# One pair of head sums taken by VectorE alone, and the order of several steps moved, in a gated cross-attention and low-rank expert layer

## The chip, the core and the metric

The kernel runs on one core of a Trainium2 chip. The metric is the device time of the whole program in microseconds. The engines are called as the profile calls them: PE (TensorE, matrix products), DVE (VectorE), ACT (ScalarE), POOL (GpSimd), SP (SyncE, which here only issues DMAs).

## What is computed

16 batches x of 128 rows and 1024 columns go through two gated residual steps. C is 128, there are 8 heads of 64 channels, and the second step has 64 experts of rank 16.

```
n = 1024 columns; xn = layernorm(x); q, k, v projections with Wq, Wk, Wv of 512 x 128
qh = softmax(Wq xn, over the 64 channels of a head) * 64**-0.5
kh = softmax(Wk ctx, over the 1024 columns)
context = kh vh^T (64 x 64 per head);  out = Wo (context^T qh) + bo
x = x + tanh(g_xattn) * out / max(norm(out over channels), 1e-12) * g * sqrt(128)
u = layernorm(x);  scores = u Wr^T;  gates = softmax(top 16 of 64 scores), else 0
h = u A^T (64 x 16);  x = x + tanh(g_ffn) * ((h * gates) B^T) * 2
```

## The kernel before, in words

**Precision.** A float32 product is done as three passes (`three_pass`): both operands are split in a high part (suffix `_hi`, copied by ACT in a rounded type) and a low part (`_lo`, the difference, made by DVE or POOL); lines L61, L62 and L63 are the passes hi x hi, hi x lo and lo x hi. A "512-column matmul" below is one such pass of 512 columns.

**Attention part.** It is a software pipeline of 17 bodies, b = 0 to 16. Body b does the head of batch b (query and key projections in `mm_q` and `mm_k`, the two softmaxes, the transposes of both) and the tail of batch b-1 (context, fold with the weights Wv and Wo, output). Body 15 has no batch to prepare ahead, body 16 only has a tail. Each engine has its own program, written out by hand in `body`, and the engines meet at semaphores only; so the order in each engine's `body` is the order of its work. DVE runs bodies 0 and 1, a loop over 2 to 4 (with `early=True`, where `part_early(b - 2)` adds up squares for the norm), a loop over 5 to 13, and bodies 14, 15 and 16.

**Query softmax.** The 1024 values of a row (position) of a batch, in four pairs p of 128 positions x 1024 (two groups of eight heads by 64 channels), go through these steps: DVE `max_q` (L1013) takes the maximum of each head straight from PE's result, for p = 0, 1, 2 PE subtracts it by a matmul (`shift_q`, L1491), ACT `exp_q` makes `qe` (L678; p = 3 in L685 pieces with the maximum as a bias), POOL `halve` adds the two halves of each head (`qhalf`, L447), DVE `sum_q` reduces these 32 values per head (`qsum`, L1018) and takes the reciprocal (`qrec`, L1021), POOL multiplies (L454), PE transposes (`tr_q`, L1510), ACT and DVE split the transposed tile (`hi_q`, `lo_q`, L693 and L1027). Keys: `max_k` (L1007), `exp_k` (L670), `tr_k` (L1501), `hi_k` (L700), `lo_k` (L1038).

**Tail.** `context` (PE) gives kc; `hi_kc` (ACT) and `lo_kc` (DVE, L1043) split it; `fold` (PE) needs `kc_lo`; `scale_m` (DVE, L1055) scales; `mt_hi` (ACT), `mt_lo` (POOL, L546); `output` (PE) needs `mt_lo` and `qT_lo`; `out_o` (ACT, L728) copies out. In body 0 there is also the fold of the output weights: `wvo_hi` (ACT, L867) and `wvo_lo` (DVE, L1304), each in two copies. `spread` (DVE, L1003) broadcasts the row norms by a transpose, `stats2_sums` (L1071, L1073) and `std2` make the second layer norm's mean and deviation of a batch.

**FFN part.** Fifteen bodies, b = 1 to 15 (`ffn_body`), each with `up(b)` (72 passes), the column sums of a later batch (`sum_u`, L1566, from DVE's `part`), and `down(b-1)`. DVE's work around them: `norm_steps` (11 small steps of an inverse square root for the output norm), `lo_moved_h`, `turn_y` (transpose `u_in`), `route` in 11 `route_step`s (top 16 of the scores and their softmax; step 2 releases ACT's `exp_scores`, L811), `gated` and `turn_h` (L1145, L1178). ACT then moves strips (`y_raw`, `h_raw`, L778, 32x256 each), and POOL does the residual addition from `rb` (L525, L528). The third body (`third`, b = 3) has an order of its own in DVE's program.

## Time and profile before

| | |
|---|---|
| Time, median of 3 runs | 920.5 us (919.33 to 921.06) |
| The profiled execution | 921.38 us |
| Its span, first to last instruction | 919.5 us |
| Mean granted TensorE clock | 0.996 |
| PE busy (share of the span) | 898.3 us (98%) |
| DVE, ACT, POOL busy | 737.2 (80%), 680.6 (74%), 520.1 (57%) |
| Chain that ended last, by engine | PE 63%, DVE 16%, ACT 7%, issue 7%, POOL 5% |

How to read it: the share of an engine is over the whole span. PE is 98% busy, so about 21 us of the span are time in which PE waits, in some fifteen places; every other engine has much more idle time, which costs nothing as long as PE is not waiting for it. The timeline rows below give start, length, engine, source line, operation, tiles and shapes, and in brackets how long the engine was idle before and who released it.

### The profile page before, as it was taken

Reading aid. Unit: us, or ns where it says so; the run is one execution under the profiler, and the core shown is the slowest. Engines: PE = TensorE matmul, PEld = TensorE weight load, DVE = VectorE, ACT = ScalarE, POOL = GpSimd, SP = SyncE. Lnnn points to the kernel's source line nnn. Section 1 sums busy time; section 2 is a strip of 40 time slices with the busy share of each in tenths; the row PEclk is TensorE's granted clock in tenths of the full one; section 3 lists DMA queues with packets and bytes.
Section 4 is the critical chain, followed back from the end, with each engine's and each line's share of the span. In section 5 each row is a group of like instructions: output and inputs, shape, how many; then the busy total and the mean of one; then the engine's idle time right before and its main releaser. Section 6 shows DMA issues by size and latency. Waiting matters only on the chain.

```text
span 919.5 us, 15914 instructions
## 1 busy us (share of the span) xinstructions
PE 898.3 (98%) x4732; PEld 760.7 (83%) x4732; DVE 737.2 (80%) x1531; ACT 680.6 (74%) x1392; POOL 520.1 (57%) x342
## 2 busy tenths in 40 slices
PE   7899999999999999999999999999999999999998
PEld 5687887878888888888887799988899989999996
DVE  6888899888888888888887878897877768777642
ACT  4787787687678768777877748678888878888731
POOL 3686777788798789879778958231222212222100
PEclk9999999999999999999999999999999999999999
DMA  4323524443453544344232694112222111212001
GB/s 160 115 82 129 178 78 156 163 144 111 161 185 108 168 139 127 109 135 156 91 115 69 207 354 165 67 68 69 76 71 70 67 64 69 70 67 69 24 24 46
DMA packets 35325, 104.09 MB, mean 113 GB/s; under 512 B 4432, under 2 KB 11600, under 8 KB 35280
## 3 DMA queue, kind: packets, MB, share of 16 engines
q1 hardware_dynamic: 29520, 82.59, 26.2%
q0 software_dynamic: 5472, 20.45, 7.5%
q10 hardware_dynamic: 288, 0.52, 0.1%
q8 instruction: 19, 0.31, 0.1%
q14 instruction: 26, 0.21, 0.1%
HBM read 79.43 MB, written 24.12 MB: 113 GB/s over the span
## 4 chain that ended last, share of the span: by engine, by line
PE 63%; DVE 16%; issue 7%; ACT 7%; POOL 5%; DMA 1%; ACTq 0%; DVEq 0%; POOLq 0%
PE ps L61 19%; PE ps L63 18%; PE ps L62 18%; PE ps L1501 4%; PE ps L1510 3%; DVE qmax L1013 2%; ACT h_raw L778 2%; DVE kmax L1007 2%; PE ps L1491 2%; DVE qT_lo L1027 1%; DVE mt L1055 1%; ACT y_raw L778 1%; ACT qT_hi L693 1%; POOL x L528 1%; POOL qe L454 1%
## 5 line engine op out<-in xcount | busy, mean ns | idle before, releaser
L525 POOL TENSOR_TENSOR rb<-u_in,rb 128x1024 f32<-128x1024 f32 x14 | 33.7, 2410 | 219.0 <-DVE rb L1003 219.0
L454 POOL TENSOR_TENSOR qe<-qe,qrec 128x1024 f32<-128x1024 f32 x64 | 121.2, 1903 | 28.9 <-DVE qrec L1021 28.9
L61 PE MATMUL ps<-aT_hi,yT_hi 128*128 128x448 f32 (+2 forms) x360 | 119.9, 333 | 1.8 <-DVE hg L1145 1.3
L62 PE MATMUL ps<-aT_hi,yT_lo 128*128 128x448 f32 (+2 forms) x360 | 118.7, 330 | 0.0
L63 PE MATMUL ps<-aT_lo,yT_hi 128*128 128x448 f32 (+2 forms) x360 | 118.6, 330 | 0.0
L1027 DVE TENSOR_TENSOR qT_lo<-ps,qT_hi 128x512 fp32r<-128x512 f32 x128 | 82.1, 683 | 42.6 <-ACT qT_hi L693 42.6
L778 ACT ACTIVATE h_raw<-hg 32x256 f32<-32x256 f32 x248 | 103.0, 415 | 17.0 <-DVE hg L1178 14.2
L447 POOL TENSOR_TENSOR qhalf<-qe 128x512 f32<-128x512 f32 x64 | 82.3, 1286 | 32.7 <-ACT qe L685 30.8
L778 ACT ACTIVATE y_raw<-u_in 32x256 f32<-32x256 f32 x216 | 89.5, 414 | 5.8 <-DVE u_in L1161 3.5
L61 PE MATMUL ps<-bT_hi,hT_hi 128*128 128x512 f32 x240 | 93.7, 390 | 0.0
L62 PE MATMUL ps<-bT_hi,hT_lo 128*128 128x512 f32 x240 | 93.5, 390 | 0.0
L63 PE MATMUL ps<-bT_lo,hT_hi 128*128 128x512 f32 x240 | 93.4, 389 | 0.0
L678 ACT ACTIVATE qe<-ps 128x1024 f32<-128x1024 f32 x48 | 49.2, 1025 | 46.4 <-PE ps L1491 46.4
L693 ACT ACTIVATE qT_hi<-ps 128x512 fp32r<-128x512 f32 x128 | 70.7, 598 | 14.9 <-PE ps L1510 13.6
L1007 DVE TENSOR_REDUCE kmax<-ps 128x1 f32<-128x1024 f32 x64 | 77.9, 1216 | 4.0 <-PE ps L63 2.4
L670 ACT ACTIVATE ek<-ps,kmax 128x1024 f32<-128x1024 f32 x64 | 72.3, 1130 | 4.7 <-DVE kmax L1007 3.0
L61 PEld LDWEIGHTS ps<-aT_hi,yT_hi 128*128 128x128 f32 x360 | 68.5, 190 | 5.0 <-issue 1.7
L1510 PE MATMUL ps<-ident,qe 128*128 128x128 f32 x512 | 69.1, 275 | 1.7 <-DVE ekT_lo L1038 1.5
L62 PEld LDWEIGHTS ps<-aT_hi,yT_lo 128*128 128x128 f32 x360 | 68.4, 190 | 2.1
L63 PEld LDWEIGHTS ps<-aT_lo,yT_hi 128*128 128x128 f32 x360 | 68.5, 190 | 1.8
L1510 PEld LDWEIGHTS ps<-ident,qe 128*128 128x128 f32 x512 | 58.0, 140 | 14.0 <-DVE ekT_lo L1038 3.3
L700 ACT ACTIVATE ekT_hi<-ps 128x512 fp32r<-128x512 f32 x100 | 54.5, 601 | 16.0 <-PE ps L1501 16.0
(180 smaller groups left out, 2556.3 us busy)
## 6 DMA issues: line engine op xcount, KB each, us to landing
x_in<-in_x SPq DMA_DIRECT2D x16, 512.0 KB, 4.2
ctx_in<-in_ctx SPq DMA_DIRECT2D x16, 512.0 KB, 4.7
ctxT_in<-in_ctxT SPq DMA_DIRECT2D x16, 512.0 KB, 3.3
ctxT_hi<-in_ctxT POOLq DMA_DIRECT2D x16, 512.0 KB, 3.7
u_scratch<-osb SPq DMA_DIRECT2D x16, 512.0 KB, 2.9
x<-in_x SPq DMA_DIRECT2D x15, 512.0 KB, 4.0
out<-res SPq DMA_DIRECT2D x15, 512.0 KB, 2.9
turn_scratch<-ek SPq DMA_DIRECT2D x14, 512.0 KB, 5.7
```

The source lines that it names most:

```text
L61: nc.tensor.matmul(psum, whi, mhi, start=start, stop=False)
L62: nc.tensor.matmul(psum, wlo, mhi, start=False, stop=False)
L63: return nc.tensor.matmul(psum, whi, mlo, start=False, stop=stop)
L447: nc.gpsimd.tensor_tensor(qhalf[:, p % 2, :].rearrange("p (h d) -> p h d", d=DH // 2), v[:, :, 0:DH // 2], v[:, :, DH // 2:DH], ALU.add).t ...
L454: nc.gpsimd.tensor_tensor(v, v, w, ALU.mult).then_inc(q_norm, 1)
L670: nc.scalar.activation(to, of, ACT.Exp, bias=kmax[:, j:j + 1], accum_out=ksum[:, j:j + 1]).then_inc(k_exp, 1)
L693: nc.scalar.activation(qT[0][:, :, n * P:n * P + P], psT[:, h, :].rearrange("p (j n) -> p j n", n=P), ACT.Copy).then_inc(q_hi, 1)
L700: nc.scalar.activation(ekT[0][:, 4 * h:4 * h + 4, j * P:j * P + P], psT[:, h, :].rearrange("p (n d) -> p n d", d=P), ACT.Copy).then_inc(k_ ...
L778: last = nc.scalar.activation(dst[32 * q:32 * q + 32, 256 * a:256 * a + 256], src[32 * a:32 * a + 32, 256 * q:256 * q + 256], ACT.Copy)
L1007: nc.vector.tensor_reduce(kmax[:, j:j + 1], psK, axis=AX.XY, op=ALU.max, negate=True).then_inc(k_max, 1)
L1027: nc.vector.tensor_tensor(qT[1][:, :, v], psT[:, h, :].rearrange("p (j n) -> p j n", n=P), qT[0][:, :, v].bitcast(f32), ALU.subtract).then ...
L1510: last = nc.tensor.transpose(psT[:, h, j * P:j * P + P], qe[:, p, w:w + P], ident[:, :])
```

## The change

It has seven parts.

1. POOL's `halve(b-1, 3)` is gone; DVE's `sum_q` for p = 3 reduces the 1024 exponentials in `qe` itself, once it has them from ACT, in place of 512 half sums.
2. In DVE's bodies 1 to 14, `sum_q(b-1, 3)` stays in its place, `max_q(b, 0)` comes ahead of `lo_kc(b-1)`, and `early_guess` (body 14 only) behind `max_q`. In the loop over bodies 2 to 4 `part_early` moves from behind `lo_k(b, 1)` to behind `max_k(b, 1)`. Body 1 has no `part_early`.
3. In body 0, ACT's `wvo_hi` goes behind `exp_q(0, 2)`, and DVE's `wvo_lo` (`low_fold`) behind `lo_k(0, 2)`, ahead of `max_q(0, 3)`.
4. In body 15, both `spread`s, `sum_q(14, 3)` and `stats2_sums(0, 0)` move on DVE, and `scale_first` and `normalise(0, 0)` on ACT; the latter goes to body 16.
5. In body 16 `sum_q` comes ahead of `lo_kc`, and PE does `tr_q(15, 1)` ahead of `tr_y(0, 0)`.
6. In body 14 PE's `sum_early` comes behind both halves of `context`.
7. In DVE's third FFN body the first three steps of `route(3)` go to the front and all eleven steps of the next norm behind `turn_y(4, 0)`.

The core of the diff (the pieces are in this order: POOL's body; ACT's body; DVE's sum, body and FFN body; PE's body 16, then its others):

```diff
-                if tail:
-                    halve(b - 1, 3)
...
             def body(b, head, tail, ahead, early=False):
                 if tail:
                     exp_q(b - 1, 3)
+                if tail and not head:
+                    normalise(0, 0)
                 if head:
                     hi_xn(b, 1)
+                if tail:
+                    hi_kc(b - 1)
                 if head and not ahead:
                     scale_first(0)
-                if tail:
-                    hi_kc(b - 1)
...
+                if head:
+                    hi_k(b, 1)
+                    exp_k(b, 3)
+                if tail:
+                    hi_q(b - 1, 3)
                 if head and not ahead:
                     scale_first(1)
-                if head:
+                if tail and head:
+                    out_o(b - 1, 0, early)
+                if head:
+                    exp_q(b, 2)
                     if not started(b):
                         act.wait_ge(fold_done, 1)
...
-                    hi_k(b, 1)
-                    exp_k(b, 3)
-                if tail:
-                    hi_q(b - 1, 3)
-                    if head:
-                        out_o(b - 1, 0, early)
-                if head:
-                    exp_q(b, 2)
...
             def sum_q(b, p):
-                dve.wait_ge(q_half, 4 * b + p + 1)
-                nc.vector.tensor_reduce(qsum[:, p, :], qhalf[:, p % 2, :].rearrange("p (h d) -> p h d", d=DH // 2),
-                                        axis=AX.X, op=ALU.add).then_inc(q_sum, 1)
+                if p == 3:
+                    dve.wait_ge(q_exp, 8 * b + 8)
+                    whole = qe[:, 3, :].rearrange("p (h d) -> p h d", d=DH)
+                else:
+                    dve.wait_ge(q_half, 3 * b + p + 1)
+                    whole = qhalf[:, p % 2, :].rearrange("p (h d) -> p h d", d=DH // 2)
+                nc.vector.tensor_reduce(qsum[:, p, :], whole, axis=AX.X, op=ALU.add).then_inc(q_sum, 1)
...
                 if ahead and started(b):
                     stats(b + 1)
-                if norms:
-                    early_guess()
                 if ahead and started(b):
                     std(b + 1, range(3))
-                if tail and ahead:
-                    sum_q(b - 1, 3)
                 if tail:
-                    lo_kc(b - 1)
-                if tail and not head:
                     sum_q(b - 1, 3)
                 if head and started(b):
                     max_q(b, 0)
+                if norms:
+                    early_guess()
+                if tail:
+                    lo_kc(b - 1)
+                if head and started(b):
                     max_k(b, 1)
-                if last:
-                    sum_q(b - 1, 3)
-                if last:
-                    dve.wait_ge(ctx_lo, 2 * NB)
-                    spread(0, rb_first[0], n_newton, 4 * NEWTON)
+                if early:
+                    part_early(b - 2)
...
                 if tail:
                     scale_m(b - 1)
+                if last:
+                    dve.wait_ge(ctx_lo, 2 * NB)
+                    spread(0, rb_first[0], n_newton, 4 * NEWTON)
...
-                if last:
-                    dve.wait_ge(xn_lo, 2 * NB)
-                    spread(1, rb_first[1], n_newton, 4 * NEWTON)
-                if early:
-                    part_early(b - 2)
...
+                if last:
+                    dve.wait_ge(xn_lo, 2 * NB)
+                    spread(1, rb_first[1], n_newton, 4 * NEWTON)
                 if ahead:
                     max_k(b + 1, 0)
+                if head and not last:
+                    sum_q(b, 1)
+                if head:
+                    lo_k(b, 2)
+                if not started(b):
+                    low_fold()
                 if last:
                     stats2_sums(0, 0)
-                if head:
                     sum_q(b, 1)
-                    lo_k(b, 2)
...
                 elif third:
-                    norm_steps(5, range(7))
+                    for n in range(3):
+                        route_step(3, n)
                     lo_moved_h(2)
                     turn_y(4, 0)
-                    norm_steps(5, range(7, NRT))
-                    route(3)
+                    norm_steps(5, range(NRT))
+                    for n in range(3, TOP):
+                        route_step(3, n)
                     spread_u(5)
...
-                    tr_y(0, 0)
                     tr_q(b - 1, 1, next(turn))
+                    tr_y(0, 0)
...
-                if isinstance(b, int) and b == NB - 2:
-                    sum_early()
                 if tail:
                     context(b - 1, 0)
                     context(b - 1, 1)
+                if isinstance(b, int) and b == NB - 2:
+                    sum_early()
```

How it moves instructions, at three places. First the loop over bodies 2 to 4 on DVE, from the last sum of the batch before to the first transposed query tile (rows of register and wait instructions are left out). Before:

```order
L1018 TENSOR_REDUCE qsum<-qhalf 128x16
L1021 RECIPROCAL qrec<-qsum 128x16
L1043 TENSOR_TENSOR kc_lo<-ps,kc_hi 128x512
L1013 TENSOR_REDUCE qmax<-ps 128x16
L1007 TENSOR_REDUCE kmax<-ps 128x1
L1027 TENSOR_TENSOR qT_lo<-ps,qT_hi 128x4x128
...
L969 TENSOR_REDUCE part<-osq 128x32
```

Now:

```order
L1021 TENSOR_REDUCE qsum<-qe 128x16
L1023 RECIPROCAL qrec<-qsum 128x16
L1011 TENSOR_REDUCE qmax<-ps 128x16
L1045 TENSOR_TENSOR kc_lo<-ps,kc_hi 128x512
L1005 TENSOR_REDUCE kmax<-ps 128x1
L967 TENSOR_REDUCE part<-osq 128x32
L1029 TENSOR_TENSOR qT_lo<-ps,qT_hi 128x4x128
```

The maximum stands ahead of `kc_lo`, the sum reads `qe`, and `part` (which stood some 35 rows further down, behind `ekT_lo`) now stands between the key maximum and `qT_lo`. In the loop over bodies 5 to 13 the rows are the same without `part`.

The second place is DVE in body 15, from the fourth query pair's transposed tile to the third key tile's low part (`rb_first1` is the broadcast of the second norm, `bn2` and `mv2` are `stats2_sums`). Before:

```order
L1003 STREAM_TRANSPOSE rb_first1_101<-nr_86 128x1024
L1027 TENSOR_TENSOR qT_lo_68<-ps,qT_hi_67 128x4x128 x2
L1323 RECIPROCAL krec<-ksum 128x4
L1071 BN_STATS bn2<-x2_0_105 128x6 x2
L1073 BN_AGGR mv2<-bn2 128x2
L1018 TENSOR_REDUCE qsum<-qhalf_73 128x16
L1021 RECIPROCAL qrec<-qsum 128x16
L1038 TENSOR_TENSOR ekT_lo_66<-ps,ekT_hi_65 128x4x128 x2
L76 TENSOR_SCALAR s1<-mv2 128x1
```

Now:

```order
L1029 TENSOR_TENSOR qT_lo_68<-ps,qT_hi_67 128x4x128 x2
L1322 RECIPROCAL krec<-ksum 128x4
L1001 STREAM_TRANSPOSE rb_first1_101<-nr_86 128x1024
L1040 TENSOR_TENSOR ekT_lo_66<-ps,ekT_hi_65 128x4x128 x2
L1083 BN_STATS bn2<-x2_0_105 128x6 x2
L1085 BN_AGGR mv2<-bn2 128x2
L1021 TENSOR_REDUCE qsum<-qhalf_73 128x16
L1023 RECIPROCAL qrec<-qsum 128x16
L76 TENSOR_SCALAR s1<-mv2 128x1
```

The broadcast stands behind `qT_lo` and `krec`, and the statistics and the sum behind `ekT_lo`.

The third place is DVE at the start of the third FFN body (`sc`, `top8` and `neg_top` are the first three steps of the routing, `ns`, `nr` and `nt` those of the norm). Before:

```order
L984 TENSOR_TENSOR nt_87<-nr_86,ns_85 128x32
L986 SCALAR_TENSOR_TENSOR nt_87<-nt_87,nr_86 128x32
L1191 TENSOR_TENSOR hT_lo_114<-h_raw_117,hT_hi_113 128x1024
L1161 STREAM_TRANSPOSE u_in0_103<-u_in0_103 128x1024
L988 SCALAR_TENSOR_TENSOR nr_86<-nt_87,nr_86 128x32
L984 TENSOR_TENSOR nt_87<-nr_86,ns_85 128x32
L986 SCALAR_TENSOR_TENSOR nt_87<-nt_87,nr_86 128x32
L988 SCALAR_TENSOR_TENSOR nr_86<-nt_87,nr_86 128x32
L1098 COPY sc_123<-ps 128x64
L1101 MAX top8<-sc_123 128x8
L1104 TENSOR_SCALAR neg_top<-top8 128x1
```

Now:

```order
L1110 COPY sc_123<-ps 128x64
L1113 MAX top8<-sc_123 128x8
L1116 TENSOR_SCALAR neg_top<-top8 128x1
L1203 TENSOR_TENSOR hT_lo_114<-h_raw_117,hT_hi_113 128x1024
L1173 STREAM_TRANSPOSE u_in0_103<-u_in0_103 128x1024
L978 TENSOR_SCALAR ns_85<-ps 128x32
L67 TENSOR_SCALAR nr_86<-ns_85 128x32
L982 TENSOR_TENSOR nt_87<-nr_86,ns_85 128x32
```

The three steps of the routing now stand ahead of `hT_lo` and of the transposition of `u_in0`, and all eleven of the norm behind them.

## Rows read from the trace of the kernel before

**Rows 1.** POOL by line: tiles, shapes, xcount, then busy us, mean ns, idle before

```profile
L447 POOL TENSOR_TENSOR qhalf<-qe 128x512 f32<-128x512 f32 x64 | 82.3, 1286 | 32.7 <-ACT qe L685 30.8 <-ACT qe L678 1.8
```

**Rows 2.** DVE timeline, steady body: start, length, engine, line, operation, [idle before]

```profile
302.62 0.69 DVE L1018 TENSOR_REDUCE qsum<-qhalf 128x16 f32<-128x512 f32 x1
303.51 0.65 DVE L1043 TENSOR_TENSOR kc_lo<-ps,kc_hi 128x512 fp32r<-128x512 f32 x1
304.20 1.22 DVE L1013 TENSOR_REDUCE qmax<-ps 128x16 fp32r<-128x1024 f32 x1
...
307.82 1.29 DVE L1027 TENSOR_TENSOR qT_lo<-ps,qT_hi 128x512 fp32r<-128x512 f32 x2 [1.04 <-ACT qT_hi L693]
```

**Rows 3.** Timeline of PE, same body

```profile
303.77 0.39 PE L63 MATMUL ps<-wq_lo,xn_hi 128*128 128x512 f32 x1
...
305.48 0.70 PE L1491 MATMUL ps<-qmax,ident_r 128*128 128x512 f32 x2
...
306.81 0.36 PE L61 MATMUL ps<-wvo_hi,kc_hi 128*128 128x256 f32 x1
```

**Rows 4.** Timeline of POOL, same body

```profile
311.17 1.27 POOL L546 TENSOR_TENSOR mt_lo<-mt,mt_hi 128x512 fp32r<-128x512 f32 x1 [2.35 <-ACT mt_hi L715]
```

**Rows 5.** Timeline of DVE in an early body (b = 2)

```profile
114.82 1.29 DVE L1027 TENSOR_TENSOR qT_lo<-ps,qT_hi 128x512 fp32r<-128x512 f32 x2 [1.27 <-ACT qT_hi L693]
...
127.13 1.23 DVE L969 TRANSPOSE_TENSOR_REDUCE part<-osq 128x1024 f32 x1
```

**Rows 6.** Timeline of PE, same early body

```profile
112.48 0.48 PE L1491 MATMUL ps<-qmax,ident_r 128*128 128x512 f32 x1 [0.33 <-DVE qmax L1013]
```

**Rows 7.** Timeline of DVE in body 0

```profile
30.06 1.28 DVE L1304 SCALAR_TENSOR_TENSOR wvo_lo<-ps,wvo_hi 128x512 fp32r<-128x512 f32 x2
```

**Rows 8.** Timeline of PE in body 0

```profile
30.33 0.50 PE L61 MATMUL ps<-ctx_hi,wk_hi 128*128 128x512 f32 x1 [1.27 <-ACT ek L670]
...
38.11 0.63 PE L1510 MATMUL ps<-ident,qe 128*128 128x128 f32 x4 [1.16 <-DVE ekT_lo L1038]
```

**Rows 9.** PE by stretches: stretch, length, PE busy (instructions), granted clock, DMA share, GB/s

```profile
31.00:34.00 3.00, 3.00 (x11) 0.50 0.09 29
...
655.40:658.80 3.40, 3.40 (x12) 0.50 0.61 206
```

**Rows 10.** Timeline of DVE in body 15

```profile
516.58 1.25 DVE L1071 BATCH_NORM_STATS2 bn<-x 128x6 f32<-128x512 f32 x2
...
518.94 1.22 DVE L1038 TENSOR_TENSOR ekT_lo<-ps,ekT_hi 128x512 fp32r<-128x512 f32 x2
...
521.84 1.28 DVE L1038 TENSOR_TENSOR ekT_lo<-ps,ekT_hi 128x512 fp32r<-128x512 f32 x2
```

**Rows 11.** Timeline of ACT in body 15

```profile
517.25 1.09 ACT L700 ACTIVATE ekT_hi<-ps 128x512 fp32r<-128x512 f32 x2
```

**Rows 12.** Timeline of PE in body 15

```profile
505.61 0.50 PE L61 MATMUL ps<-qT_hi,mt_hi 128*128 128x512 f32 x1 [1.21 <-POOL mt_lo L546]
...
522.66 0.52 PE L1510 MATMUL ps<-ident,qe 128*128 128x128 f32 x3 [0.38 <-DVE ekT_lo L1038]
```

**Rows 13.** Timeline of ACT in the third FFN body

```profile
614.68 0.35 ACT L811 ACTIVATE ex<-sc,neg_top 128x64 f32<-128x64 f32 x1 [2.83 <-DVE neg_top L1104]
614.94 6.81 ACT L778 ACTIVATE y_raw<-u_in 32x256 f32<-32x256 f32 x16
...
622.82 2.54 ACT L778 ACTIVATE h_raw<-hg 32x256 f32<-32x256 f32 x6
```

**Rows 14.** Timeline of DVE in the third FFN body

```profile
613.31 0.19 DVE L984 TENSOR_TENSOR nt<-nr,ns 128x32 f32<-128x32 f32 x1
...
619.58 1.25 DVE L1178 STREAM_TRANSPOSE hg<-hg 128x1024 f32<-128x1024 f32 x1
```

**Rows 15.** Timeline of PE, third and fourth FFN bodies

```profile
624.54 0.47 PE L61 MATMUL ps<-aT_hi,yT_hi 128*128 128x448 f32 x1 [0.41 <-DVE yT_lo L1173]
...
654.85 0.40 PE L1566 MATMUL ps<-part,sel 128*128 128x32 f32 x2 [2.14 <-DVE part L1209]
```

## What the change does to the time: a prediction

> **What bounds the kernel now.** I read the table of engines first. PE is busy in 98% of the span, so the whole change can only add to, or take from, some 21 us of PE's waits, and work moved between DVE and POOL has no effect by itself. Next come the waits of PE and who ended them, and then, in each body that the change touches, the timelines of DVE, ACT and POOL around those waits. In a steady body (b = 5 to 13) PE hardly waits: there the reader is to see which engine was ready last at each meeting. The rest of PE's waits are in body 0, in bodies 2 to 4, in 15, and in the third and fourth FFN bodies, and each of these has edits of its own.
>
> **Part 1, the sum of the fourth pair.** POOL loses 16 additions of 1.29 us, 20.6 us in all [rows 1], and DVE reduces 1024 values where it reduced 512. The reduction of 512 takes 0.69; no 1024-wide sum stands in the trace, but a maximum of the same shape takes 1.22 [rows 2], from PE's output memory, so I take 1.22 to 1.25: 0.53 more, 16 times, 8.5 us of DVE work. The bounds for its length are 0.69 (no dearer than before) and 1.38 (twice the half). What of this lies on the path? In the steady body DVE starts the sum at 302.62 and the query maximum at 304.20; but PE's last pass for that maximum starts at 303.77 and lasts 0.39, until 304.16 [rows 2, 3]. The maximum thus starts when PE releases it, not when DVE is ready. Before, what followed sum and reciprocal (`kc_lo`, 303.51) began 0.89 after the sum. Now the maximum follows them, so it could begin at 302.62 + 0.89 + 0.53 = 304.04, with 0.12 to spare. With 1.38 that is 304.20, when it began before. So PE's shift at 305.48 stays, and the chain behind it. **Cost 0** for nine bodies, bounds 0 and +0.1 each.
>
> `kc_lo` is made behind the maximum instead: it ends at 305.42 + 0.65, about 306.05, and the fold that wants it starts at 306.81 [rows 3]: 0.7 to spare. The key maximum behind it comes 0.5 to 0.6 later, into DVE's idle time of 1.04 ahead of `qT_lo` [rows 2]. POOL's saved 1.29 us ends ahead of `mt_lo`, for which POOL already waited 2.35 on ACT [rows 4]: no gain. Body 14 is like these; `early_guess` there is two small steps between the maximum and `kc_lo`, within the same 0.7, and `sum_early` only changes its place on PE: 0.
>
> The Trainium skill speaks against this part: "VectorE: DVE Perf Modes", Rules for kernel authors, says of `tensor_reduce` on a hot path to expect the plain rate, calls it the slowest operation of that engine, and advises to restructure. By that rule, taken as a cost on the path, the sum would be 16 times 0.53, or 8.5 us, slower; the trace has DVE free in time in every steady body, and I go by the trace.
>
> **Part 2, bodies 2 to 4.** There the query maximum is already late: PE waits 0.33 for it [rows 6]. Before, the sum, the reciprocal and `kc_lo` stood ahead of it; now a sum longer by 0.53 stands there and `kc_lo` (0.55 per step) doesn't. Equal. But `part` (1.23; 1.16 from its start to the next one's, as neighbours overlap) now stands between the key maximum and `qT_lo`, with `kc_lo` also moved there. DVE's idle time was 1.27 [rows 5]. Of it `kc_lo` takes 0.5 and `part` 1.16, sum 1.66, so `qT_lo`, `mt` and all behind come 0.39 later, which I read as PE time since the output in this body waits for the chain of `mt`. Later in the body 1.16 is free where `part` was, but behind the chain. Three bodies: **+1.1**, bounds 0 (if the chain has slack that the rows don't show) and +1.6.
>
> **Part 3, body 0.** ACT copies the key tile and makes the exponentials some 1 us earlier, so PE's wait of 1.27 at 30.33 gets about 0.6 shorter; the second half of that product still waits for POOL's low part of ctx near 31.0. But DVE's `low_fold` (1.28 for both, a step of 1.18 [rows 7]) now stands between `ekT_lo` and the last maximum and last `ekT_lo`, for which PE waits already, 1.16 at 38.11 [rows 8]. So +1.2 there, less what comes from the earlier start, and about 0.4 from the half-clock stretch that goes with this wait: from 31.0 to 34.0 the granted clock was 0.50, the lower level of 1.2 GHz, after a wait [rows 9], and eleven instructions filled 3.0 us. Net **+0.2**, bounds -0.5 and +0.7.
>
> **Parts 4 and 5, bodies 15 and 16.** `spread(0)` comes behind `scale_m`, so the first output, for which PE waited 1.21 on POOL at 505.61, is ready 0.8 earlier [rows 12]. It isn't kept. ACT's copy of the third key tile begins at 517.25 [rows 11], its first half is ready near 517.9, and it is late because of what is ahead of it on ACT. Before, DVE filled the time until 518.94 with the statistics, sum 1 and the reciprocal, 2.36 us from 516.58 on [rows 10]. Now these stand behind `ekT_lo`, which can't start before 517.9: DVE idles ahead of it, and the 2.36 us come afterwards. The last `ekT_lo` was 2.90 after the third tile's [rows 10]; now it is 517.9 + 2.90 + 2.36 = 523.2 where it was 521.84, so `tr_q(15, 0)` moves from 522.66 [rows 12] to 524.0. That is +1.3. In body 16 the transposes of PE in the other order give back about 0.25. Net **+1.0**, bounds -0.8 (ACT is also earlier, the gain kept) and +1.4.
>
> **Part 7, the third FFN body.** ACT waited 2.83 for `neg_top` and began `y_raw` at 614.94, only behind `exp_scores` [rows 13]. With the routing's three steps in front, `exp_scores` goes at about 612, and `y_raw` starts once `u_in` is transposed, at 613.24: 1.70 earlier. Not all is kept: behind the transposition DVE now has seven more steps of the norm, of 0.19 and a gap each [rows 14], 1.5 us, and three of the routing less, 0.9; so `turn_h`, 619.58 before, comes 0.5 to 0.7 later, and `h_raw` starts at about 621.7 for 622.82 [rows 13]. That is **-1.14**. PE sees it in two steps: the wait of 0.41 at 624.54 goes, and of the 2.14 at 654.85 some 0.6 [rows 15]. Bounds -0.41 (only the first wait) and -1.7.
>
> Behind the wait of 2.14 the clock stood at 0.50 from 655.4 on, again the lower level, for 3.4 us in which PE was busy throughout [rows 9]: at full clock the same work takes 1.7. The wait shrinks to 1.5 or 1.6. The wait of 1.21 at 505.61 [rows 12] was followed by no such stretch; that of 1.27 at 30.33 was, though with other waits just ahead of it. The row nearest to 1.6 says neither clearly; I take it that it goes: **-1.5**, bounds 0 and -1.7.
>
> **Sum.** +1.1 + 0.2 + 1.0 - 1.14 - 1.5 = -0.3 us. The profiled execution (921.38 with a span of 919.5) lies 0.9 above the median of 920.5; its waits are those of any execution, so I take the difference off the median: 920.2.
>
> **Rivals.**
> - *A half-clock stretch stays or appears.* PE's new wait ahead of `tr_q(15, 0)` is 2.5 us by the working above (the 0.8 won and the 1.3 lost and the old 0.38), longer than the one before 655.4. For: that one was followed by the lower clock, and the wait here comes behind earlier ones in the same body. Against: the wait falls apart if some passes run in between. It costs 1.6: -0.3 + 1.6 = +1.3, 921.8. The stretch at 655.4 staying gives +1.2, 921.7; both +2.8, 923.3.
> - *DVE becomes the bound in the steady bodies* (ending slower). It decides where the reduction takes over 1.34 (1.22 and the 0.12 to spare); from there each 0.1 costs nine bodies 0.1 each. At 1.54: +1.8 on -0.3, 922.0. For: the margin is thin. Against: maxima of that width are steady at 1.22.
> - *The change gains more.* If ACT's copy in body 15 is earlier too, since `scale_first(1)` no longer stands ahead of `hi_k`, the 1.3 isn't lost and 0.8 is kept: -0.3 - 2.1 = -2.4, 918.1. Against: its other work, and PE's transposes that it waits for, stand where they were.
> - *It doesn't do what it says.* If the routing's steps wait for PE's scores where they now stand, `exp_scores` goes no earlier, and neither the -1.14 nor the -1.5 comes: -0.3 + 2.6 = +2.3, 922.8. Against: the scores belong to the batch of this body and DVE read them at once when it came to them.
>
> **How the numbers follow.** Chances: my forecast with no stretch of low clock in 15, and none at 655, 0.40 (919.3 to 921.2); a stretch in body 15 alone 0.22; that at 655 alone 0.15; both 0.07; DVE as the bound in steady bodies 0.04; nothing from the FFN body 0.03; more gain 0.09. The range from 918.2 to 923.0 takes in all but the end of "both" and the far ends of the others. About 0.2%, 1.84 us, is what a measurement can tell here, 918.7 to 922.3 is "same". Faster: more gain (0.09) and the low end of the forecast (0.06), 0.15. Slower: both stretches (0.07), DVE as bound (half, 0.02), nothing from the FFN (0.03), and the high ends of the two single stretches, which with the bounds of parts 2 and 3 pass 922.3 (0.11): 0.23. Same: 0.62.
>
> **What would show it.** Steady bodies: period unchanged, the query maximum released by PE, DVE's idle time ahead of `qT_lo` about 0.5. Bodies 2 to 4: no idle time of DVE ahead of `qT_lo`, each body 0.4 longer. Body 0: PE's wait ahead of `tr_q` near 2, the other shorter. Body 15: DVE idle about 1 ahead of the third `ekT_lo`, PE's wait ahead of `tr_q(15, 0)` over 2. FFN: no wait at 624, the one before `sum_u` at 1.6, the clock at 1.00 behind it. It is wrong if the 1024-wide sum is over 1.4, if bodies 2 to 4 keep their length, or if body 15 is not longer.

## The result, and the profile after

The changed kernel takes 926.57 us (924.04 to 927.45, 5 runs) against 920.5 us (919.33 to 921.75): the ratio is 1.0055, with a 95% interval of 1.0037 to 1.0073. It is **slower by 0.55%**, where 920.2 us was forecast and the range ended at 923.0. The profiled execution of the changed kernel took 926.57 us, its span 924.7 us, at a mean granted clock of 0.994 (0.996 before).

The page of the changed kernel, its span and its engines (busy us, share of the span, instructions), and the groups of DVE that answer to [rows 1, 2]:

```profile
span 924.7 us, 15908 instructions
PE 900.6 (97%) x4732; PEld 761.7 (82%) x4732; DVE 745.6 (81%) x1531; ACT 680.3 (74%) x1392; POOL 501.2 (54%) x326
...
L1021 DVE TENSOR_REDUCE qsum<-qhalf 128x16 f32<-128x512 f32 x48 | 32.5, 678 | 0.8 <-POOL qhalf L447 0.4
L1021 DVE TENSOR_REDUCE qsum<-qe 128x16 f32<-128x1024 f32 x16 | 19.4, 1211 | 2.2 <-ACT qe L683 2.2
```

POOL has 16 instructions and 19 us less, DVE 8.4 us more, and the 1024-wide sum takes 1.21 us, as taken in the prediction. That part of the change did what it says. Where the 5.2 us between the two spans arose is read from the starts of the first pass of `context` on PE, body by body:

| stretch | before, us | after, us | difference |
|---|---|---|---|
| start to the context of body 1 | 39.0 | 40.0 | +1.0 |
| body 1 | 31.8 | 33.4 | +1.6 |
| bodies 2 to 4 | 98.0 | 98.4 | +0.4 |
| bodies 5 to 12 | 256.5 | 256.4 | -0.1 |
| bodies 13 and 14 | 64.0 | 64.4 | +0.4 |
| body 15 | 34.2 | 35.9 | +1.7 |
| body 16 and the FFN part | 395.9 | 396.2 | +0.3 |

Of the first row 0.7 is no effect of the change: PE's first projection starts at 9.89 us for 9.17, since the first load landed later (over all profiles of this case that start lies between 9.1 and 10.1 us, whatever the order). The steady bodies are as long as before. In one of them the query maximum is still released by PE, now with 0.16 us of idle time of DVE ahead of it (to set against [rows 2]):

```profile
305.44 1.21 DVE L1021 TENSOR_REDUCE qsum<-qe 128x16 f32<-128x1024 f32 x1
306.68 0.25 DVE L1023 RECIPROCAL qrec<-qsum 128x16 f32<-128x16 f32 x1
307.10 1.22 DVE L1011 TENSOR_REDUCE qmax<-ps 128x16 fp32r<-128x1024 f32 x1 [0.16 <-PE ps L63]
308.24 0.68 DVE L1045 TENSOR_TENSOR kc_lo<-ps,kc_hi 128x512 fp32r<-128x512 f32 x1
```

The loss sits at the two ends of the attention part, where PE waits for DVE's low part of a key tile. PE of the changed kernel, to set against [rows 8, 12, 15]; the third group is the column sums in the FFN part:

```profile
39.05 1.16 PE L1518 MATMUL ps<-ident,qe 128*128 128x128 f32 x8 [2.36 <-DVE ekT_lo L1040]
...
508.00 0.50 PE L61 MATMUL ps<-qT_hi,mt_hi 128*128 128x512 f32 x1 [0.40 <-POOL mt_lo L544]
...
527.55 1.16 PE L1518 MATMUL ps<-ident,qe 128*128 128x128 f32 x8 [2.63 <-DVE ekT_lo L1040]
...
660.43 0.40 PE L1574 MATMUL ps<-part,sel 128*128 128x32 f32 x2 [1.97 <-DVE part L1221]
```

Shortly behind each of the three long waits, PE worked at half clock. The same view as [rows 9] (stretch, its length, PE busy and instructions, granted clock, DMA share, GB/s):

```profile
40.80:43.80 3.00, 3.00 (x8) 0.50 0.00 0
528.40:531.90 3.50, 3.50 (x12) 0.53 1.00 245
661.60:664.80 3.20, 3.20 (x13) 0.53 0.48 161
```

Before, there were two such stretches, at 31 and at 655 us; now there are three, at 41, 528 and 662. At half clock a pass of 512 columns takes 427 ns instead of 227, so that a stretch of 3.4 us costs PE about 1.6 us. PE is never idle in them, which is why the waits alone don't show this loss. Body 1 holds the first, the beginning of body 16 the second.

### The profile page after: what moved, and what is told of

The parts are those of the page before. It is cut to its first block, busy times and chain, and to the rows that moved or that the text cites. A ratio compares the mean times of both kernels' runs of the same rounds, so it can differ in the third digit from the quotient of the medians.

```text
span 924.7 us, 15908 instructions
## 1 busy us (share of the span) xinstructions
PE 900.6 (97%) x4732; PEld 761.7 (82%) x4732; DVE 745.6 (81%) x1531; ACT 680.3 (74%) x1392; POOL 501.2 (54%) x326
## 4 chain that ended last, share of the span: by engine, by line
PE 72%; DVE 15%; ACT 6%; issue 5%; POOL 1%; DMA 1%; ACTq 0%; DVEq 0%; POOLq 0%
PE ps L61 21%; PE ps L63 20%; PE ps L62 20%; PE ps L1518 5%; PE ps L1509 4%; ACT h_raw L776 3%; DVE kmax L1005 2%; PE ps L1499 2%; DVE qmax L1011 1%; DVE mt L1067 1%; DVE qT_lo L1029 1%; DVE qsum L1021 1%; DVE bn L947 1%; ACT qT_hi L691 1%; DVE ekT_lo L1040 1%
## 5 line engine op out<-in xcount | busy, mean ns | idle before, releaser
L447 POOL TENSOR_TENSOR qhalf<-qe 128x512 f32<-128x512 f32 x48 | 61.6, 1282 | 12.7 <-ACT qe L676 12.7
```

Source lines behind the costliest of these rows:

```text
L447: nc.gpsimd.tensor_tensor(qhalf[:, p % 2, :].rearrange("p (h d) -> p h d", d=DH // 2), v[:, :, 0:DH // 2], v[:, :, DH // 2:DH], ALU.add).t ...
```

## The experiments

Theory A was: DVE's moved steps make two new long waits of PE (body 0 and body 15), and the chip answers each with a stretch at its lower clock; the rest are small waits in bodies 2 to 4 and 14. The rival was that the wider sum, DVE's greater load, costs it. The comparisons share runs of the kernel before, with medians of 920.7 to 921.2 us.

**Undoing body 0 and undoing body 15.** The first run takes part 3 out of the changed kernel:

```diff
                 if head:
+                    if not started(b):
+                        act.wait_ge(fold_done, 1)
...
                     hi_k(b, 1)
...
                 if head:
                     exp_q(b, 2)
-                    if not started(b):
-                        act.wait_ge(fold_done, 1)
...
                                                 ALU.mult, ALU.mult).then_inc(gcol_done, 1)
+                        low_fold()
...
                     lo_k(b, 2)
-                if not started(b):
-                    low_fold()
```

> The changed kernel with part 3 undone: wvo_hi and wvo_lo stand in body 0 where they stood before. Theory A (PE's new wait of 2.36 us ahead of tr_q(0, 0), made by DVE's low_fold, and the stretch of half clock right behind it): the wait goes back to about 1.2 us, the stretch at 41 to 44 us is gone but the old one at 31 to 34 us comes back, so body 0 is about 0.3 us shorter and body 1 1.6 us shorter: 924.6 us for 926.57. Theory B (the wider sum and DVE's greater load cost it): no change within 0.5 us, and body 1 stays at 33.4 us.

It took 923.72 us (921.91 to 925.27, 7 runs), 2.85 less than the changed kernel; against before 1.0029 (1.0017 to 1.0041). PE's wait and the clock, from its trace:

```profile
38.07 1.17 PE L1517 MATMUL ps<-ident,qe 128*128 128x128 f32 x8 [1.16 <-DVE ekT_lo L1040]
```

```profile
30.00:34.00 4.00, 2.76 (x16) 1.00 0.46 137
38.00:44.00 6.00, 5.93 (x30) 1.00 0.42 168
```

The wait is back at 1.16, and body 1 at 31.8 us. The old stretch at 31 us did not come back, though: theory A had the place right and the gain too small, because it took for given a stretch that only the profile of before has: the seven others with that order in body 0 lack it. (The execution in the profile took 925.27 us; its stretch at the end of body 15 was twice as long as usual.)

The second run puts the statistics and the second sum of body 15 back:

```diff
-                if head and not last:
+                if last:
+                    stats2_sums(0, 0)
+                if head:
                     sum_q(b, 1)
-                if head:
                     lo_k(b, 2)
...
-                if last:
-                    stats2_sums(0, 0)
-                    sum_q(b, 1)
```

> The changed kernel with one edit of body 15 undone: stats2_sums(0, 0) and sum_q(15, 1) stand ahead of lo_k(15, 2) again; the two broadcasts stay moved. Theory A (DVE idles 1.05 us ahead of the third ekT_lo and does these 2.4 us afterwards): PE's wait ahead of tr_q(15, 0) falls from 2.63 to under 1 us, body 15 is 1.5 to 2.4 us shorter, and no stretch of half clock follows, 1.6 us more: 922.6 to 923.5 us. Theory B (the moves on ACT or the broadcasts made the wait): the wait stays over 2 us, and the time at 926.

It took 923.28 us (920.44 to 924.93, 8 runs), 3.3 less: theory A. PE and DVE of that run:

```profile
523.14 1.16 PE L1507 MATMUL ps<-ident,ek 128*128 128x128 f32 x8 [0.78 <-DVE ekT_lo L1040]
...
526.08 0.63 PE L1516 MATMUL ps<-ident,qe 128*128 128x128 f32 x4 [0.39 <-DVE ekT_lo L1040]
```

```profile
520.00 1.24 DVE L1083 BATCH_NORM_STATS2 bn<-x 128x6 f32<-128x512 f32 x2
...
522.36 1.22 DVE L1040 TENSOR_TENSOR ekT_lo<-ps,ekT_hi 128x512 fp32r<-128x512 f32 x2
```

The long wait has become two of 0.78 and 0.39, and no half clock follows. What holds the rest of body 15's loss (34.7 us for 34.2) is not settled: with the second broadcast behind `qT_lo`, DVE idles 0.84 us ahead of `qT_lo`, but the run with part 1 alone (below) has 34.7 us too, with both broadcasts in their old place.

**The wait and the clock apart.** Eight idle matmuls fill PE's wait of body 15 in the changed kernel; nothing reads their result.

```diff
+                if head and not ahead:
+                    for k in range(8):
+                        nc.tensor.matmul(psK[:, 0, :], ident_r[:, :],
+                                         ident_r[:, :].unsqueeze(1).broadcast_to([P, 4, P]), start=True, stop=True)
                 if head:
                     tr_q(b, 0, next(turn))
```

> The changed kernel with eight matmuls more on PE (128x128 by 512, of no use, into the key tile's output memory, which nobody reads any more) ahead of tr_q(15, 0), that is inside PE's wait of 2.63 us there. They last 1.8 us at full clock. Theory A (the stretch of half clock behind 528 us comes from PE having stood still): the wait for DVE ends at the same moment, but the granted clock stays 1.00 behind it, and the time is 1.5 us less, 925.0 us. Theory B (the clock falls for another reason, such as the DMA traffic of over 250 GB/s there): the stretch stays, and the time too.

It took 923.29 us (921.67 to 924.53, 12 runs), 3.3 less than the changed kernel, with all of its useful work in the same order. PE and the windows of that run:

```profile
523.82 1.98 PE L1708 MATMUL ps<-ident_r 128*128 128x512 f32 x8
526.64 1.16 PE L1518 MATMUL ps<-ident,qe 128*128 128x128 f32 x8 [0.84 <-DVE ekT_lo L1040]
```

```profile
527.50:531.00 3.50, 3.50 (x18) 1.00 1.00 286
527.60:537.00 9.40, 9.11 (x55) 1.00 0.98 325
```

Body 15 still lasts 35.9 us, so the wait for DVE is as long as before, but the clock stays at 1.00 with 286 GB/s of DMA traffic beside it: the traffic is not the cause (the stretch at 41 us had none beside it either), the standing still is. That is 1.6 us of the gain. The clock fits the rest too: 11 of the 12 executions had a mean granted clock of 0.998, as one stretch leaves it (half clock for 3.4 of some 920 us), while the five of the changed kernel had 0.992 to 0.996, two to four stretches. The stretch in the FFN part was missing in this profile, although the wait ahead of the column sums was as long as ever. That was not expected, and shows that such a wait makes a stretch likely, not certain; why filling the wait of body 15 should make a later stretch rarer stays open.

**Part 3 alone.** The edit of the first run, done to the kernel before.

> The kernel before with part 3 alone (wvo_hi and wvo_lo later in body 0). Theory A: PE's wait ahead of tr_q(0, 0) grows from 1.16 to 2.4 us, the context of body 1 starts 0.3 us later than before (less what the first loads differ), and a stretch of half clock at 40 to 44 us replaces the one at 31 to 34 us, which not every run of before has: +0.3 to +1.9 us, 922.3 us if half of the runs of before have that stretch. Theory B (part 3 harms only together with the wide sum): 921 us and no stretch at 41.

923.44 us (921.3 to 924.44, 8 runs), 1.0025 (1.0013 to 1.0037): slower than before by 2.7 us of the medians, without the wide sum.

```profile
38.59 1.16 PE L1511 MATMUL ps<-ident,qe 128*128 128x128 f32 x8 [2.36 <-DVE ekT_lo L1038]
```

```profile
39.60:42.60 3.00, 3.00 (x10) 0.53 0.01 3
```

Wait and stretch are those of the changed kernel. The cost has two parts of like size. The first is seen against a profile with the old order of body 0 that has no stretch there, that of part 7 alone (further down). Its first pass of the query projection and its first pass of the context:

```profile
13.64 0.47 PE L61 MATMUL ps<-wq_hi,xn_hi 128*128 128x512 f32 x1 [1.39 <-POOL xn_lo L433]
...
39.02 0.48 PE L61 MATMUL ps<-ekT_hi,ctxT_hi 128*128 128x512 f32 x1
```

and those of this run:

```profile
12.95 0.48 PE L61 MATMUL ps<-wq_hi,xn_hi 128*128 128x512 f32 x1 [1.42 <-POOL xn_lo L433]
...
39.51 0.56 PE L61 MATMUL ps<-ekT_hi,ctxT_hi 128*128 128x512 f32 x1
```

From one to the other it is 26.56 us here and 25.38 there: part 3 makes body 0 longer by 1.2 us. The profile of before hides this, because its own stretch at 31 us makes the same distance 26.36. The second part is the stretch in body 1, 1.6 us (33.39 us for 31.8); together that is 2.8, near the 2.7 of the medians. In this profile a wait of 0.96 us at 568 us, which the kernel before lacks, adds to it; it was not followed up.

**Part 1 alone.** The wide sum, `halve` gone, and `max_q` ahead of `kc_lo` in bodies 1 to 14, nothing else.

> The kernel before with part 1 alone and the order of max_q ahead of kc_lo that goes with it: POOL's halving of the fourth pair is gone, DVE sums 1024 values. early_guess, part_early and all of bodies 0, 15 and 16 (but for the sum) stay as before. Theory A: bodies 5 to 12 keep 32.06 us, bodies 2 to 4 gain or lose under 0.1 us each, body 14 loses 0.4 us, since there the wide sum and the two small steps ahead of max_q are together too long: 921.5 us. Theory B (the wider sum costs its 0.53 us in every body): 929 us.

921.79 us (919.62 to 922.66, 12 runs), 1.0008 (0.9998 to 1.0018): the same as before. Bodies 5 to 12 take 32.06 us each (32.07 before), and the rival of 0.53 us a body is refuted. Bodies 2 to 4 are 0.15 us shorter each (32.72, 32.37, 32.39), and bodies 14 and 15 longer by 0.3 and 0.5. In body 14 `early_guess` stands ahead of the maximum, and with the wide sum PE waits for that:

```profile
464.71 0.48 PE L1495 MATMUL ps<-qmax,ident_r 128*128 128x512 f32 x1 [0.26 <-DVE qmax L1011]
...
504.84 0.50 PE L61 MATMUL ps<-qT_hi,mt_hi 128*128 128x512 f32 x1 [1.73 <-POOL mt_lo L544]
...
655.05 0.40 PE L1570 MATMUL ps<-part,sel 128*128 128x32 f32 x2 [2.42 <-DVE part L1211]
```

The last row is worth a look. The wait of 2.42 is the longest at this place in any run, and the clock behind it stayed at 1.00.

**Bodies 2 to 4.** `part_early` back in its old place in the changed kernel.

> The changed kernel with part_early of bodies 2 to 4 back behind lo_k(b, 1). The three bodies took 33.03, 32.65 and 32.69 us from context to context, for 32.87, 32.54 and 32.55 before. Theory A (part took DVE's idle time ahead of qT_lo, as predicted, only with less harm): they go to 32.87, 32.54 and 32.55. Theory B (part_early is only moved from one full place of DVE to another): they stay.

One run took 925.74 us; the bodies took 32.68, 32.39 and 32.40 us, below the 32.87, 32.54 and 32.55 of before. So the moved `part` costs 0.3 us a body, and `max_q` ahead of `kc_lo` gains 0.15, as in the run before this one.

**Body 14.** `early_guess` and `sum_early` back in the changed kernel:

```diff
+                if norms:
+                    early_guess()
                 if ahead and started(b):
                     std(b + 1, range(3))
```

> The changed kernel with early_guess back ahead of the small steps on DVE in body 14, and PE's sum_early back ahead of the context. In the changed kernel the second instruction of early_guess, an integer step of 96 columns, took 1.15 us while POOL was multiplying, for 0.21 us before, and kc_lo and PE's fold (a wait of 0.38) came late. Theory A (it is held up by POOL's multiplication): the step takes 0.2 us, the wait ahead of the fold at 470 us is gone, bodies 13 and 14 together are 0.4 us shorter, 926.2 us. Theory B (the wide sum makes kc_lo late): the wait stays.

925.73 us (924.65 to 927.18, 5 runs). Bodies 13 and 14 took 64.4 us together, as in the changed kernel: the wait only moved from the fold to the shift. Both theories are half right, as DVE's step was shorter than in the changed kernel, but not back at 0.2 us. The step that was long is the integer step of 96 columns, which ends each time with POOL's instruction. The changed kernel, DVE and then POOL:

```profile
468.76 1.15 DVE L67 TENSOR_SCALAR nr<-ns 128x96 int32<-128x96 int32 x1
469.84 0.68 DVE L1045 TENSOR_TENSOR kc_lo<-ps,kc_hi 128x512 fp32r<-128x512 f32 x1
```

```profile
466.08 3.77 POOL L454 TENSOR_TENSOR qe<-qe,qrec 128x1024 f32<-128x1024 f32 x2
```

And this run:

```profile
464.74 0.72 DVE L67 TENSOR_SCALAR nr<-ns 128x96 int32<-128x96 int32 x1
```

```profile
464.10 1.29 POOL L433 TENSOR_TENSOR xn_lo<-xn,xn_hi 128x512 fp32r<-128x512 f32 x1 [4.60 <-ACT xn_hi L642]
```

466.08 + 3.77 is 469.85 and 468.76 + 1.15 is 469.91; here 464.10 + 1.29 is 465.39 and 464.74 + 0.72 is 465.46. In the kernel before, the step took 0.21, since POOL's instruction ended with it.

**Part 7 alone**, in the kernel before.

> The kernel before with part 7 alone, the new order of DVE in the third FFN body. Theory A (y_raw is 1.7 us earlier, h_raw 1.2, and of that 0.8 is lost again where POOL's second addition takes 3.2 us instead of 2.4): the wait at 624 us is gone, the one ahead of the column sums at 655 us is 1.9 to 2.0 us, 0.9 us gained, 919.6 us, and the stretch of half clock behind it stays. Theory B, my prediction's step: the stretch goes too, 918.1 us.

918.74 us (917.93 to 919.99, 11 runs), 0.9975 (0.9966 to 0.9984): **faster than before**. From PE's resumption at 600.6 us to the column sums it is 52.84 us for 54.09, so 1.25 us gained, and the wait of 0.41 at 624 us is gone. The medians differ by 2.4, and the clock fits the rest: all of the 11 executions had a mean granted clock of 0.997 or more, where 11 of the 20 of before had 0.997 or less; no trace shows where the stretches stood that went. But the one at this place is still there:

```profile
653.41 0.40 PE L1568 MATMUL ps<-part,sel 128*128 128x32 f32 x2 [1.63 <-DVE part L1209]
```

```profile
654.60:657.90 3.30, 3.30 (x12) 0.51 0.45 159
```

Even a wait of 1.63, just what the prediction had for this place, was followed by half clock here.

**Four undone together**: the changed kernel without part 3, with the statistics of body 15, `early_guess`, `sum_early` and `part_early` back.

> The changed kernel with four of its edits undone together: part 3 (body 0), stats2_sums and sum_q(15, 1) in body 15, early_guess and sum_early (body 14), and part_early (bodies 2 to 4). The wide sum, the broadcasts, body 16, ACT's moves and part 7 stay. Theory A (the losses are these four, each in its place): 926.57 less 2.9, 3.3, 0.1 and 0.9, that is 919.4 us, like before or a little less. Theory B (the remaining parts, the wide sum above all, hold some of the loss): over 921 us.

920.18 us (918.63 to 921.81, 12 runs), 0.9991 (0.9982 to 1.0). The four edits hold 6.4 us, all of the loss of 6.1 and a little more; the single runs gave 2.85, 3.3, 0.8 and 0.8, more than the whole; that each median also depends on how often a stretch falls where would explain it, but is not shown. The median is 0.8 above theory A. The profiled execution, the slowest with 921.81, had half clock from 12 to 18 us as well, ahead of anything that the change touches.

**A better order.** The kernel before with part 7, the first broadcast behind `scale_m`, the new order of PE in body 16, `sum_early` behind the context, and `early_guess` split in two (`early_root` is its integer step):

```diff
                     max_q(b, 0)
+                    if norms:
+                        early_guess()
                     max_k(b, 1)
+                    if norms:
+                        early_root()
```

> The kernel before with what is expected to gain: part 7 (third FFN body); the first broadcast of body 15 behind scale_m; tr_q(15, 1) ahead of tr_y(0, 0); PE's sum_early behind the context, with early_guess split, its first step behind max_q and its integer step of 96 columns behind max_k, where DVE has idle time. The sum by halves and all else stay. Theory A: -1.2 (third FFN body), -0.4 (bodies 13 and 14), -0.5 to -0.8 (bodies 15 and 16), the sum 2.1 to 2.4 us: 918.2 us, and less where a stretch of half clock goes. Theory B (body 15 gives its gain back at its end, DVE being full there): 918.9 us.

918.64 us (917.41 to 920.28, 12 runs), 0.9976 (0.9967 to 0.9985), no better than part 7 alone. Bodies 13 to 15 are 0.6 us shorter in its profile, but a new wait for `yT_lo` in body 16 (0.47 at 531.72) takes most of it back. Theory B. The integer step took 0.85 us there, again to the end of POOL's instruction, and cost nothing, as DVE had that time.

Then the column sums of the FFN loop's first body, ahead of which PE waited, one piece later:

```diff
-                late = isinstance(i, int) and b in (1, 2, 4)
+                late = b in (1, 2, 4) if isinstance(i, int) else j == 0
```

> The kernel of run e9 with one more edit on PE: in the first body of each turn of the FFN loop (b = 5 and 9) the column sums stand behind the second piece of up(b) instead of the first. In the FFN PE waited 1.6 to 2.1 us for DVE's part ahead of them, and a stretch of half clock followed in each profile but two. Theory A (wait and stretch are both PE's loss, DVE needs the sums only 3 us later): both go, up to 3.4 us less: 915.3 us. Theory B (DVE and ACT set the pace there, so that PE waits later instead): the wait turns up again within one body, but in smaller pieces that no half clock follows: 917 us. Theory C: no change, 918.6 us.

**916.19 us** (915.58 to 916.74, 5 runs), 0.9954 (0.994 to 0.9967): the fastest, 4.5 us below before. Its trace has one wait of 0.26 left in that region, and full clock:

```profile
674.71 0.40 PE L1574 MATMUL ps<-part,sel 128*128 128x32 f32 x2 [0.26 <-DVE part L1213]
```

```profile
649.00:655.00 6.00, 6.00 (x34) 1.00 0.39 127
655.00:660.00 5.00, 5.00 (x37) 1.00 0.15 61
```

From 600 us to the end its profile is 3.6 us shorter than that of run e9, theory A's size; the medians differ by 2.45, between theories A and B, as not every execution of e9 has the stretch. The three executions of each with a granted clock of 1.0 throughout (917.4 to 917.8 and 915.6 to 916.2 us) differ by 1.8, about the wait alone. The wide sum on top:

> The kernel of run e11 with part 1 on top, the wide sum, and max_q ahead of kc_lo in the bodies 1 to 14; part_early, early_guess, bodies 0 and 15 stay as in e11. Theory A (the wide sum is free in the steady bodies and gains 0.15 us in each of bodies 1 to 4): 0.5 us less than e11. Theory B (DVE's margin is gone, and what it gains there it loses in bodies 14 and 15, 0.3 and 0.5 us): the same as e11 or 0.3 us more.

917.06 us (916.36 to 918.01, 6 runs), 0.9965 (0.9952 to 0.9977). Theory B: bodies 2 to 4 keep their 0.15 us each, but in the profile body 15 is 0.2 us longer and two waits behind it are 0.3 and 0.6 longer, and that is more.

## Why the prediction was wrong, step by step

**Part 1, the sum in the steady bodies: right.** 1.21 us for 1.22 to 1.25, a margin of 0.16 for 0.12, and no change in eight bodies. The rule of the Trainium skill that speaks against a reduction on the hot path ("VectorE: DVE Perf Modes", Rules for kernel authors) would have given 8.5 us more; the run with part 1 alone gave none that can be measured, because DVE's extra work lay in idle time. One small cost came with it all the same. In the FFN part, ahead of one broadcast `rb<-nr`, DVE idles 0.46 us in all nine profiles of kernels with the wide sum and 0.11 in the five without; the changed kernel:

```profile
646.38 1.25 DVE L1001 STREAM_TRANSPOSE rb<-nr 128x1024 f32<-128x1024 f32 x1 [0.46 <-DVE nr L986]
```

The column sums behind it come 0.35 us later for it (54.45 us from PE's resumption at 600 us with part 1 alone, 54.09 before). What holds DVE there is not shown.

**Part 2, bodies 2 to 4: mechanism right, size off.** Each was 0.1 to 0.2 us longer, not 0.39. `part` costs 0.3, near to what was said, but the step "Equal" for the maximum was wrong: with `kc_lo` behind it, the maximum came earlier than before by 0.15.

**Body 14 "the same 0.7": wrong.** `early_guess` was priced as two small steps. One of them took 1.15 because POOL was at work, `kc_lo` came late, and the fold waited 0.38.

**Part 3: the +0.2 came out by luck, and its consequence was left out.** The new wait of 2.36 is the 1.16 and the 1.2 of the text, and between the two profiles the net cost up to `tr_q(0, 0)` was 0.94 less the 0.72 of the first load, the forecast +0.2. But the two terms taken off were both wrong. The earlier start gave nothing: PE's wait for ACT fell from 1.19 to 0.77, and then PE waited at 35 us for an `ekT_lo` that came when it always had. And the stretch at 31 us, priced at 0.4, had cost 1.0 in the one profile that has it (26.36 us for 25.4), and most profiles of the old order have nothing to lose there. Nor did the prediction ask whether the longer wait at 39 would bring a stretch of its own. It did, and kernels with and without part 3 differ by 2.7 to 2.85 us: 1.2 for the body and 1.6 for the stretch.

**Part 4: right in its place, too small.** The text has DVE idle ahead of the third `ekT_lo` and the statistics behind it; the trace has 1.05 us of idle time there. `tr_q(15, 0)` was forecast 1.3 us later than before, and a wait of 2.5; it is 1.7 later within the body, with a wait of 2.63. ACT's copy of the key tile started 0.3 later than assumed, behind `scale_first(1)`. The stretch of half clock behind it was the first rival, with 0.22 and 0.07; it came in all four profiles that have this wait unfilled. **This is the step that failed most**: the longest wait of the kernel was in the text, longer than the one that it knew to be followed by half clock, and still the likelier case was "no stretch", so that the sum has nothing for it where the trace has 1.6 us. With the wait filled, the time fell by 3.3.

**Part 7: the first half right, the second wrong.** `y_raw` came 1.69 us earlier (1.70 forecast), `h_raw` 1.29 (1.14), the wait at 624 went; the column sums came 0.91 earlier (1.14), and 1.25 with part 7 alone: the difference is the 0.35 of part 1 above. The rest of what `y_raw` gained was lost where POOL's second addition took 3.20 us instead of 2.40, in both kernels, and DVE waited for it. The Trainium skill bears on that ("SBUF — State Buffer", Who interferes with whom): a VectorE instruction with two inputs in SBUF contends with a GpSimd one that reads SBUF. In the trace that addition starts while `yT_lo`, an instruction of that kind, runs. The -1.5 for the stretch did not come: the wait was 1.97, and the run with part 7 alone shows that the forecast 1.6 is no shelter either.

**The sum.** Forecast -0.3: 0 + 1.1 + 0.2 + 1.0 - 1.14 - 1.5. Measured between the two profiles: 0.7 (first load), 0.2 (body 0), 0.4 (bodies 2 to 4), 0.4 (bodies 13 and 14), 1.7 (body 15), -0.9 (third FFN body), -0.5 (the rest), and 3.2 for two stretches of half clock in new places; the 0.2 is 1.2 for part 3 less the 1.0 of the stretch at 31 us, which only one of eight profiles with the old order has. The forecast had -1.5 for the clock in the FFN part, -0.4 in body 0 and nothing for new stretches. No case had three stretches, and so the range ended 3.6 us too low.

## What to carry to other kernels

Where PE is nearly always busy, a wait of PE that grows to some 2 us, as here, has two prices, the wait and the slower work behind it, and here the second (1.6 us) was as large as the first (1.2 and 1.7): price both for every wait that an edit lengthens, not only for those that had it before. Work taken from a step on the path and put "where the engine idles" must fit the idle time ahead of what PE waits for next; statistics for a later stage belong ahead of an operand that comes late anyway, not behind it. A stretch of the lower clock in one profile is one draw: look at several executions or several kernels before counting on its being there or on its going, and compare a distance between two profiles only when both or neither have a stretch inside it.

## What the runs showed of the hardware that was not expected

**The lower clock came by chance, and behind waits of 1.6 to 2.6 us more often than not.** All stretches had the granted clock at 0.50, which is 1.2 GHz of 2.4. Behind the wait ahead of the column sums at 653 to 661 us (1.6 to 2.4 us) a stretch followed in 10 of 12 profiles; the two without it had waits of 1.95 and 2.42, no shorter than the others. With the unfilled wait of 2.6 us in body 15 it came in 4 of 4 (in one it began 0.7 us before the wait ended), behind that of 2.1 to 2.4 in body 0 in 4 of 6, and in the other two a stretch stood at 32 us instead, behind a wait of only 0.7 to 0.8. With the order of before, whose waits there are 1.2 to 1.3, only 1 of 8 profiles had one between 28 and 44 us. The run with the idle matmuls shows that it is PE's standing still that matters and not the traffic.

**A stretch costs the kernel less than it costs PE, where PE would have waited anyway.** PE loses about 1.6 us in one. But of the 78 executions of the kernel before that were run beside the experiments, the 17 with a mean granted clock of 0.999 or 1.0 have a median near 919.5 us, the 27 with 0.998 (one stretch) 920.5 and the 30 with 0.996 (two) 921.7: 1.1 us a stretch. In body 0 it was 1.0 (26.36 us for 25.4), as the wait of 0.59 us at 35 us was gone in the profile with the stretch.

**A small integer step of VectorE can wait for GpSimd's instruction to end.** `nr<-ns`, 128x96, took 0.21 us in the kernel before and 0.72, 1.15 and 0.85 in three others, each time up to 0.06 to 0.08 us behind the end of the instruction that POOL was executing. The Trainium skill has a rule that fits ("SBUF — State Buffer", Who interferes with whom): `tensor_scalar`, which this step is, can enter a mode that needs the port pair shared with GpSimd; whoever issues first has that pair for the whole instruction, and the other blocks fully. The traces agree to within 0.1 us; that the step runs in that mode, no run shows.
